# Four heads' transposed probabilities evicted by one instruction in a windowed-attention kernel

## What is computed

```python
h = shift_token(x); q, k, v = split(h @ wqkv, 3)      # 8 heads of 64
q = l2norm(q) * qs; k = l2norm(k) * ksc; q, k = rotary_xpos(q, k)
# windows of 128 queries; keys are the window's own 128 and the 128 before
sim  = einsum('bhwid,bhwjd->bhwij', bq * 8, bk)        # 128 x 256 per head
attn = softmax(where(mask, -max, sim)); out = einsum('bhwij,bhwjd->bhwid', attn, bv)
x = x + out @ wo
```

## Time and profile before

| What | us |
|---|---|
| median of 3 runs | 2107.81 |
| lowest and highest run | 2107.7 and 2108.52 |
| span of the profiled execution | 2108.3 |
| TensorE busy in it | 1823.9 |
| VectorE busy | 1438.1 |
| ScalarE busy | 977.4 |
| GpSimd busy | 799.5 |

### The profile page before, as it was taken

How to read it: one execution, slowest core, us unless ns; L and a number is a source line. 1 busy time by engine, 2 the same in 40 slices (tenths; PEclk the granted TensorE clock), 3 DMA queues, 4 the chain that set the end, 5 groups by cost and what they waited for, 6 DMA issues and landing times.

```text
span 2108.3 us, 38778 instructions
## 1 busy us (share of the span) xinstructions
PE 1823.9 (87%) x10590; PEld 1396.6 (66%) x10590; DVE 1438.1 (68%) x4211; ACT 977.4 (46%) x2550; POOL 799.5 (38%) x963
## 2 busy tenths in 40 slices
PE   3868669993999999999799995999999999799990
PEld 1222448772777777777588874777777777578870
DVE  3664436675888888888755554888888888655554
ACT  1110105452677677777522212777767777422220
POOL 4000024565333333333345553333433333444545
PEclk8879779996999999999899997999999999899995
DMA  3100001112000000000010002000000000100005
GB/s 115 50 0 0 0 0 56 61 64 84 11 4 4 4 5 4 4 5 4 13 49 10 10 10 58 4 4 5 4 4 5 4 4 5 54 7 9 9 10 164
DMA packets 58388, 48.23 MB, mean 23 GB/s; under 512 B 9957, under 2 KB 56313, under 8 KB 58361
## 3 DMA queue, kind: packets, MB, share of 16 engines
q1 hardware_dynamic: 58360, 47.94, 7.2%
HBM read 29.05 MB, written 8.39 MB: 18 GB/s over the span
## 4 chain that ended last, share of the span: by engine, by line
PE 73%; DMA 6%; DVE 5%; SPq 5%; POOL 4%; ACT 3%; issue 3%; POOLq 1%; DVEq 0%; ACTq 0%; PEldq 0%; PEld 0%
PE bank L1157 11%; PE bank L1188 7%; PE bank L1163 5%; PE bank L1136 5%; PE bank L1179 5%; PE bank L1257 5%; PE bank L1137 4%; PE bank L1138 4%; PE bank L1258 4%; PE bank L1259 4%; SPq L438 4%; PE bank L1148 3%; PE bank L1022 3%; DMA x_in<-in_L_attn_hidden_states 2%; ACT pT L871 2%
## 5 line engine op out<-in xcount | busy, mean ns | idle before, releaser
L649 POOL TENSOR_TENSOR rnorm<-sumsq,neg_half 128x8 f32<-128x8 f32 x132 | 217.0, 1644 | 621.5 <-DVE sumsq L1567 621.5
L860 ACT ACTIVATE prob<-prob,neg_max 128x256 f32<-128x256 f32 x512 | 256.2, 503 | 161.9 <-DVE neg_max L1598 161.8
L1157 PE MATMUL bank<-kT,qT 128*128 128x256 f32 x1032 | 267.8, 383 | 1.7 <-DVE kT L1584 1.7
L936 ACT ACTIVATE gelu_sb<-bank,b_sb 114x512 f32<-114x512 f32 x96 | 66.2, 690 | 348.5 <-PE bank L1259 346.4
L1157 PEld LDWEIGHTS bank<-kT,qT 128*128 128x128 f32 x1032 | 197.3, 191 | 35.1 <-issue 2.5
L710 POOL TENSOR_TENSOR act_lo<-act_full,act_hi 114x512 fp32r<-114x512 f32 x96 | 128.2, 1336 | 204.4 <-PE bank L1274 152.9
L1136 PE MATMUL bank<-wqkv_hi,hT_hi 128*128 128x512 f32 x396 | 195.4, 493 | 2.0 <-DVE hT_lo L1543 2.0
L1188 PE MATMUL bank<-pT,v_sb 128*64 128x128 f32 x2048 | 168.3, 285 | 16.0 <-ACT pT L871 16.0
L1720 DVE SCALAR_TENSOR_TENSOR act_full<-bank,b_sb,gelu_sb 114x512 f32<-114x512 f32 x96 | 71.0, 740 | 152.3 <-PE bank L1259 152.3
L1257 PE MATMUL bank<-h_hi,w_hi 128*114 128x512 f32 (+1 forms) x384 | 156.2, 407 | 21.1 <-POOL h_lo L683 11.1
L1188 PEld LDWEIGHTS bank<-pT,v_sb 128*64 128x64 f32 x2048 | 106.5, 136 | 88.3 <-issue 57.1
(11 more groups left out here) (226 smaller groups left out, 4289.0 us busy)
## 6 DMA issues: line engine op xcount, KB each, us to landing
x_in<-in_L_attn_hidden_states SPq DMA_DIRECT2D x16, 512.0 KB, 3.5
hs_attn<-x_sb SPq DMA_DIRECT2D x24, 254.0 KB
raw<-in_L_ffn_wqkv SPq DMA_DIRECT2D x3, 1536.0 KB, 6.8
x_scratch<-x_in SPq DMA_DIRECT2D x8, 512.0 KB, 4.2
f_x<-x_scratch SPq DMA_DIRECT2D x8, 512.0 KB, 4.3
out<-f_y SPq DMA_DIRECT2D x8, 512.0 KB, 3.2
hs_ffn<-x_sb SPq DMA_DIRECT2D x64, 63.5 KB
raw<-in_L_ffn_w SPq DMA_DIRECT2D x2, 1364.0 KB
```

The lines of the kernel that those rows point to most:

```text
L649: pool.tensor_tensor(rnorm[:, part], sumsq[:, part], neg_half[:, part], ALU.pow).then_inc(r_ready[which], 1)
L860: act.activation(prob[:, h], prob[:, h], ACT.Exp, bias=neg_max[:, h:h + 1], scale=-1.0, accum_out=psums[:, h:h + 1]).then_inc(exped, 1)
L1157: mm = pe.matmul(bank[:, 3 + j % 2, e * 2 * P:(e + 1) * 2 * P], qT[:, j, e], kT[:, j].rearrange("p a b -> p (a b)"), start=True, stop=True)
```

## The change

The eviction of transposed probabilities becomes one ScalarE instruction for two pairs of heads: `probs_out(k, part)` reads banks 5 and 6 and writes all of pT, 128 x 1024, after both `turn_probs` of the half are done; for the second part it waits until both value groups of the first half are done. `pt_ready` counts two per block in place of four, and `turn_probs` and `values` wait for the counts that go with it. On TensorE, `project(f, 4)` moves ahead of `values(k, 0)`, so that values 0 and 1 follow each other. In the second half a new `transposes_ok(k)` waits for the second eviction, since that now reads bank 5 together with bank 6; the hidden-state transposes, which write bank 5, move behind it and ahead of `values(k, 2)`, so that values 2 and 3 follow each other too.

```diff
-                def probs_out(k, j):
-                    act.wait_ge(pt_ps, 4 * k + j + 1)
-                    if j >= 2:
-                        act.wait_ge(pv_done, 4 * k + j - 1)
-                    act.activation(pT[:, j % 2], bank[:, 5 + j % 2], ACT.Copy).then_inc(pt_ready, 1)
+                def probs_out(k, part):
+                    act.wait_ge(pt_ps, 4 * k + 2 * part + 2)
+                    if part:
+                        act.wait_ge(pv_done, 4 * k + 2)
+                    act.activation(pT[:], bank[:, 5:7], ACT.Copy).then_inc(pt_ready, 1)
...
                         weigh_odd(k, 3)
                         probs_out(k, 0)
-                        probs_out(k, 1)
                         exponent(k, 6)
                         exponent(k, 7)
                         weigh_odd(k, 5)
                         weigh_odd(k, 7)
-                        probs_out(k, 2)
-                        probs_out(k, 3)
+                        probs_out(k, 1)
                         hi(f + lay + 1)
...
                     if j >= 2:
-                        pe.wait_ge(pt_ready, 4 * k + j - 1)
+                        pe.wait_ge(pt_ready, 2 * k + 1)
...
                 def values(k, j):
-                    pe.wait_ge(pt_ready, 4 * k + j + 1)
+                    pe.wait_ge(pt_ready, 2 * k + j // 2 + 1)
...
+                def transposes_ok(k):
+                    pe.wait_ge(pt_ready, 2 * k + 2)
...
                         turn_probs(k, 0)
                         turn_probs(k, 1)
+                        project(f, 4)
                         values(k, 0)
-                        project(f, 4)
                         values(k, 1)
                         turn_probs(k, 2)
                         turn_probs(k, 3)
                         project(f, 5)
+                        transposes_ok(k)
+                        transposes(f + lay + 1)
                         values(k, 2)
-                        transposes(f + lay + 1)
                         values(k, 3)
```

## The result

The changed kernel takes 2132.28 us (median of 4 runs, 2131.02 to 2133.76) against 2107.76 us before (4 runs): a recorded ratio of 1.0127, with a 95% interval from 1.0107 to 1.0147 (the two medians divided give 1.0116, inside it). It is 24.5 us slower by the medians. The prediction was 2127.0 us in a range of 2116 to 2138: right in direction and in the half of the block that pays, 5.3 us short in size, on a forecast step of 19.2.

A forecast was written before the change was run, and what follows sets the result against it. TensorE was taken to bound each 15.64 us block. First half 0.00 and second half +0.30 us over 64 blocks gave 19.2 us; 2108.3 + 19.2 - 0.5 = 2127.0 us, range 2116 to 2138.

The forecast's parts named there:

- What bounds the kernel: Attention loop: TensorE paces 15.64 us blocks, its only other wait on the chain being for a pT eviction.
- Part 1, the width: ScalarE's pT eviction: one 1024-column instruction takes 1.02 us, saving 0.07 us per pair, none of it on the path.
- Part 2, first half: Heads 0 to 3: no change, 0.00 us, since VectorE's scaling of head 4 holds turn_probs(2).
- The reserve: First half: TensorE free at 808.61, turn_probs(2) starting at 808.90, so 0.29 us to spare.
- Part 3, second half: Heads 4 to 7: idle +0.54 us, given back 0.09 and 0.16; +0.29 per block, taken as +0.30.
- The price of leaving a value group: TensorE's switch from value matmuls to transposes: 0.15 to 0.16 us, read from gaps in the earlier trace.
- the rival built on this: Wait to turn_qk: most switch gaps vanish with grouped values, block -0.01 to +0.06 us, 2107 to 2111.5 us; chance 0.08.
- The stronger switch rival: Whole block: switches halved from eight to four, 0.5 us saved per block, 2076 us; chance 0.05.
- The clock: Attention loop: no change taken; rival has TensorE at 1.2 GHz in some blocks, 2157 us with two; chance 0.02.
- the heavy one: Grouped values no faster or the 1024-column read slower: 2137 us with one, up to 2149 with both; chance 0.15.

The follow-up runs named there:

- the run with the move alone: Kernel before with project(4) ahead of values(0), evictions kept at 512 columns: 2105.24 us, 0.9989.
- the last run: Kernel before with project(4) ahead of values(0), one 1024-column eviction in the first half only, VectorE's scaling of head 4 ahead of the sines: 2101.6 us, 0.9967.
- The narrow run: Changed kernel's TensorE order in both halves, but four 512-column evictions per block, hidden-state transposes waiting for the third: 2111.86 us, 1.0026.
- the earlier scaling of head 4: Kernel before with project(4) ahead of values(0), narrow evictions, VectorE's scaling of head 4 moved ahead of the sines: 2097.72 us, 0.9951.

## Why the prediction was right, and where its size was off

- **What bounds the kernel.** TensorE with a block of 15.64 us, and every delay behind turn_probs(2) kept whole: confirmed. The distance from turn_qk to the next block's turn_probs(0) changed by 0.02 us only (15.64 - 3.42 - 3.29 = 8.93 before, 16.03 - 3.41 - 3.71 = 8.91 after).
- **Part 1, the width.** 1.02 us was taken from another instruction's row; it measured 1.026. ScalarE's saving was 0.06 us per pair (2 x 139.0 / 256 = 1.086 us of busy time for two narrow ones with their overlap taken out, less 1.026), and no part of it arrived, as said.
- **Part 2, first half at 0.00.** 3.41 us against 3.42. The run with the move alone, the run with the wide eviction there alone, and the run with project(4) put back (+0.79 per block) show the cover and its price. The reserve was 0.23 us (3.41 against the 3.18 at which TensorE alone got there in the last run), where 0.29 was forecast.
- **Part 3, second half.** This is the term that was mis-sized: +0.30 per block, measured +0.39. The step that failed is "The extra semaphore wait of transposes_ok itself costs nothing beside the wait", together with the release of 0.04 us taken from the chain. A release that short belongs to a wait attached to the matmul it holds (0.05 us measured). A wait that stands alone with another one behind it was left only after 0.14 us. Swapping the two gave 0.09 us per block, 5.8 us in 64 blocks and 5.6 us between the medians, and the block of that run is the forecast one. That it fits to 0.01 us is in part luck: in that run the second half is 0.33 us longer than before, not 0.29 (the paired value groups take 1.03 us instead of 1.01, the release 0.05 instead of 0.04), and the first half and the rest of the block are 0.02 us shorter each.
- **The price of leaving a value group**, 0.15 to 0.16 us from the gaps in the earlier trace rows, measured 0.16 when the transposes were put back. The Trainium skill (TensorEngine Tiling (Array Packing), Key Properties) says that changing the tiling mode drains TensorE; the trace agrees with a cost for a change between the two weight forms, but the rival built on this, in which fewer switches carry the change, did not happen. Of the four switches saved, two lie in the first half, ahead of VectorE's hold, and one is the entry into values(2), which costs nothing behind an idle stretch (with the transposes put back, values(2) started 0.05 us after the eviction). One exit is left that counts.
- **Below nothing in the second half.** The stronger switch rival assumed that 0.5 us saved per block would reach the end. The narrow run shows that it would not have: there TensorE was to save 0.25 us, turn_qk started 0.18 us earlier by the trace, and both of its parts waited for VectorE's normalisations. The prediction said that VectorE "was not holding it and absorbs nothing"; true for a delay, and silent on how little room there was the other way.
- **The clock** stayed at 1.00 with TensorE busy 465.95 of 500 us, so that rival did not happen. Nor did the heavy one: the eviction measured 1.026 us, and the paired groups 1.03.

## What to carry to other kernels

Merging two evictions saved little of the engine's own time (0.06 us a pair here) and cost the latency of the wider one, from the moment the second input is full; it was free only where the consumer had other work for that long, so look at each place where it stands and count what can be moved in. When TensorE must wait for two semaphores, try the order in which the one that comes last is attached to the instruction that uses the data, and the one long satisfied stands before it (0.09 us each time, at the one place tried here). An earlier step on one engine triggers work on others: check what it will then run beside. And two versions with the same block time need not be held by the same thing: look at the chain of each.

## What the runs showed of the hardware that was not expected

- A semaphore wait that is followed by another wait released TensorE 0.14 us after the producer's end, one attached to the matmul after 0.05 to 0.06 us (changed kernel and the run with the waits swapped).
- Of a GpSimd copy of 128x128 and a VectorE product of 128x512, the one that started second was the slower for it. Copies that started during a product took 0.61 to 0.75 us instead of 0.29 and ended 0.14 to 0.15 us behind it (813.10 + 0.75 against 812.33 + 1.38 in the order without the width); the product took 0.68 us, as without a copy. A product that started with a copy still running took 0.77 us. VectorE's 0.35 us scaling beside a GpSimd addition took 0.80 to 0.92 us and ended 0.15 us behind it (811.44 + 0.92 against 810.94 + 1.27 in the changed kernel, 818.16 + 0.80 against 817.54 + 1.27 with the earlier scaling of head 4).
